# Scale and shift of the last layer norm: from GpSimd on the rows to ScalarE behind the transposes

## The reference

```python
xn = (x - mu) * rsqrt(var + EPS) * gamma + beta      # last norm, over D = 256, 6250 rows
logits = xn @ Wr + br                                # router, 8 experts
w = softmax(top_2(logits))
for e in range(8):                                   # every row only needs its two experts
    h = gelu(xn @ W1[e] + b1[e])                     # 256 -> 512
    y += (h @ W2[e] + b2[e]) * w_full[..., e]        # 512 -> 256
x = x + y
```

## Time and profile before

| what | value |
|---|---|
| time, median of 3 runs | 5023.93 us (5022.15 to 5025.44) |
| the profiled execution, its own time | 5019.38 us |
| its span, first to last instruction | 5017.7 us |
| mean granted TensorE clock | 0.823 |
| busy: PE, DVE, ACT, POOL | 64%, 59%, 39%, 56% of the span |
| heads stage | starts at 4020.1 us |
| experts stage, PE at work | from 4365.0 us |

### The profile page before, as it was taken

One profiled execution on the slowest core, in us unless ns is written; L12 is line 12 of the kernel. 1 busy time (PEld: TensorE's weight loads), 2 busy tenths in 40 slices (PEclk: granted clock), 3 DMA queues, 4 the chain that ended last, 5 costly groups with the idle time before them and its releaser, 6 DMA issues. The chain is left out here.

```text
span 5017.7 us, 69695 instructions
## 1 busy us (share of the span) xinstructions
PE 3229.1 (64%) x14347; PEld 2350.6 (47%) x14348; DVE 2974.7 (59%) x7138; ACT 1979.9 (39%) x4909; POOL 2789.1 (56%) x2929
## 2 busy tenths in 40 slices
PE   4477777777566677777798246666666532199980
PEld 1255555555454555555587134444444431066650
DVE  5677777777667777777547855555555592022223
ACT  0434444443333344444342045555555452133331
POOL 0277777677477677777450067777777645400006
PEclk9978878888778788888899668888888755599995
DMA  2433333333233333333221011111111332511115
GB/s 81 141 113 115 117 110 111 111 110 108 85 108 109 95 108 110 110 110 111 68 68 44 7 25 27 27 27 27 27 27 27 22 145 92 181 56 54 55 57 145
DMA packets 265988, 410.61 MB, mean 82 GB/s; under 512 B 77510, under 2 KB 182883, under 8 KB 265508
## 3 DMA queue, kind: packets, MB, share of 16 engines
q0 software_dynamic: 120320, 275.83, 20.6%
q1 hardware_dynamic: 145444, 132.39, 8.3%
HBM read 324.85 MB, written 83.11 MB: 81 GB/s over the span
## 5 line engine op out<-in xcount | busy, mean ns | idle before, releaser
L1482 PE MATMUL conv_ps<-conv_msg,conv_S 128*128 128x256 f32 x3328 | 1068.7, 468 | 408.5 <-DVE ACC L1492 320.8
L1482 PEld LDWEIGHTS conv_ps<-conv_msg,conv_S 128*128 128x128 f32 x3328 | 727.7, 232 | 658.3 <-DVE ACC L1492 326.7
L1458 POOL DMA_INDIRECT conv_msg<-relu_xn_table,GI x832 | 789.9, 949 | 382.9 <-issue 248.3
L1458 POOL DMA_INDIRECT conv_msg<-conv_table,GI x832 | 796.5, 957 | 326.6 <-issue 249.0
L2399 POOL DMA_INDIRECT gat_msg<-attn_table,GI x832 | 821.7, 988 | 266.2 <-issue 253.4
L1492 DVE TENSOR_TENSOR ACC<-ACC,conv_ps 128x256 f32 x1664 | 701.8, 422 | 411.8 <-issue 247.3
L2452 PE MATMUL gat_ps<-gat_M,gat_S 128*128 128x260 f32 x1664 | 598.9, 509 | 374.6 <-DVE ACC L2506 221.0
L1467 ACT ACTIVATE conv_S<-iota_row,LOC 128x128 f32<-128x128 f32 x1664 | 507.3, 388 | 530.3 <-PE conv_ps L1482 521.0
L2452 PEld LDWEIGHTS gat_ps<-gat_M,gat_S 128*128 128x128 f32 x1664 | 378.9, 246 | 517.6 <-issue 460.4
L3060 POOL DMA_INDIRECT combine_y<-expert_out,combine_at x98 | 94.6, 966 | 578.3 <-ACTq L3048 559.1
L2506 DVE TENSOR_TENSOR ACC<-ACC,gat_ps 128x260 f32 x832 | 349.7, 420 | 56.5 <-PE gat_ps L2452 23.4
(11 more groups left out here) (537 smaller groups left out, 5420.2 us busy)
## 6 DMA issues: line engine op xcount, KB each, us to landing
expert_in<-heads_zrow SPq DMA_DIRECT2D x53, 256.0 KB, 3.1
experts_xe<-expert_in SPq DMA_DIRECT2D x106, 128.0 KB
expert_out<-experts_y SPq DMA_DIRECT2D x106, 128.0 KB
conv_msg<-relu_xn_table,GI POOLq DMA_INDIRECT x832, 2.8
conv_msg<-conv_table,GI POOLq DMA_INDIRECT x832, 2.7
gat_msg<-attn_table,GI POOLq DMA_INDIRECT x832
relu_xn_table<-begin_rx SPq DMA_DIRECT2D x49, 128.0 KB, 1.7
xnT<-begin_xt SPq DMA_DIRECT2D x49, 128.0 KB, 1.8
```

The lines of the kernel that those rows point to most:

```text
L1458: pool.indirect_dma_start(self.msg[:, h * RING + k, :], None, table, bass.IndirectOffsetOnAxis(ap=self.m.GI[:, t:t + 1], axis=0)).then_inc ...
L1482: self.nc.tensor.matmul(self.ps[k % self.NB][:, 0:D], self.S[:, r % 2, k, :], self.msg[:, r % self.DEEP * RING + k, :], start=True, stop=T ...
```

## The change

`gamma` and `beta` are loaded once, as two columns of 128 (`m.gammac`, `m.betac`), in the load stage. In heads, ScalarE writes the normalised rows `xn`, which are transposed and written to DRAM without scale and shift; GpSimd keeps only the fill with zeros. Once transposed, a column of the row is a partition, so `gamma` and `beta` are per-partition operands: ScalarE's one copy of 128x256 from PSUM becomes two activations of 128x128 with scale and bias from `gammac` and `betac`. The same is done in the experts stage, whose input now comes without scale and shift. The wait for the write of a row buffer moves from GpSimd to ScalarE.

```diff
 # stage_load
-            for to, frm in ((m.b11s, m.b11), (m.b21s, m.b21)):
+            for to, frm in ((m.b11s, m.b11), (m.b21s, m.b21), (m.gammac, m.gamma), (m.betac, m.beta)):
                 load(to[:, :], frm.rearrange("(c p) -> p c", p=P), allow_slow_non_contiguous=True)
 # heads, ScalarE
                     if i >= TS:
-                        act.wait_ge(u_made, i - TS + 1)
-                    nc.scalar.activation(t[:, i % TS, :], x_of(i), ACT.Identity, scale=m.rstd[:, i:i + 1],
-                                         bias=shift[:, i:i + 1]).then_inc(t_made, 1)
+                        act.wait_ge(turned, i - TS + 1)
+                        act.wait_ge(out_xn[i % TS], i // TS * 16)
+                    nc.scalar.activation(xn[:, i % TS, :], x_of(i), ACT.Identity, scale=m.rstd[:, i:i + 1],
+                                         bias=shift[:, i:i + 1]).then_inc(xn_made, 1)
...
-                    nc.scalar.copy(xt[:, i % TS, :], pt[i % 2][:, 0:D]).then_inc(xt_made, 1)
+                    for c in range(2):
+                        op = nc.scalar.activation(xt[:, i % TS, c * P:c * P + P], pt[i % 2][:, c * P:c * P + P], ACT.Identity,
+                                                  scale=m.gammac[:, c:c + 1], bias=m.betac[:, c:c + 1])
+                    op.then_inc(xt_made, 1)
 # heads, GpSimd
             nc.gpsimd.memset(zrow[:, :], 0.0).then_inc(zeroed, 1)
-            pool.wait_ge(scales_in, 32)
-            for j in range(TILES + 1):
...
-                    nc.gpsimd.tensor_tensor(u[:, j % TS, :], t[:, j % TS, :], gammar[:, :], ALU.mult).then_inc(u_made, 1)
...
-                        pool.wait_ge(turned, i - TS + 1)
-                        pool.wait_ge(out_xm[i % TS], i // TS * 16)
-                    nc.gpsimd.tensor_tensor(xm[:, i % TS, :], u[:, i % TS, :], betar[:, :], ALU.add).then_inc(xm_made, 1)
 # heads, TensorE: wait xn_made, transpose xn;  SyncE:
-            sp.dma_start(gammar[:, :], row_to_all(m.gamma)).then_inc(scales_in, 16)
-            sp.dma_start(betar[:, :], row_to_all(m.beta)).then_inc(scales_in, 16)
...
-                sp.wait_ge(xm_made, i + 1)
-                sp.dma_start(m.xm[i * P:(i + 1) * P, :], xm[:, i % TS, :]).then_inc(out_xm[i % TS], 16)
+                sp.wait_ge(xn_made, i + 1)
+                sp.dma_start(m.xm[i * P:(i + 1) * P, :], xn[:, i % TS, :]).then_inc(out_xn[i % TS], 16)
 # experts, ScalarE
-                nc.scalar.copy(xt[s][:, :], pt[s][:, 0:D]).then_inc(xt_made, 1)
+                for c in range(2):
+                    op = nc.scalar.activation(xt[s][:, c * P:c * P + P], pt[s][:, c * P:c * P + P], ACT.Identity,
+                                              scale=m.gammac[:, c:c + 1], bias=m.betac[:, c:c + 1])
+                op.then_inc(xt_made, 1)
```

More of the change, by code:

```diff
@@ L2563, in stage_heads_to_router @@
         a, b, q, root, shift = (st.sb(n, [P, TILES]) for n in ("a", "b", "q", "root", "shift"))
-        t, u, xm, xt = (st.sb(n, [P, TS, D]) for n in ("t", "u", "xm", "xt"))
+        xn, xt = (st.sb(n, [P, TS, D]) for n in ("xn", "xt"))
         zrow = st.sb("zrow", [P, 2 * D])
-        gammar, betar = st.sb("gammar", [P, D]), st.sb("betar", [P, D])
-        scales_in = st.sem("scales_in")
         pt = [st.ps(f"pt{k}") for k in range(2)]
         pl = st.ps("pl")
-        o_made, low_made, ex_made, o_read, x_made, var_made, root_made, scaled, t_made, u_made, xm_made = (
-            st.sem(n) for n in ("o_made", "low_made", "ex_made", "o_read", "x_made", "var_made", "root_made", "scaled",
-                                "t_made", "u_made", "xm_made"))
+        o_made, low_made, ex_made, o_read, x_made, var_made, root_made, scaled, xn_made = (
+            st.sem(n) for n in ("o_made", "low_made", "ex_made", "o_read", "x_made", "var_made", "root_made", "scaled", "xn_made"))
         turned, xt_made, l_made, zeroed, zero_out = (st.sem(n) for n in ("turned", "xt_made", "l_made", "zeroed", "zero_out"))
-        out_xm = st.sems("out_xm", TS)
+        out_xn = st.sems("out_xn", TS)
         block = st.block()
@@ L2674, in _ @@
             nc.gpsimd.memset(zrow[:, :], 0.0).then_inc(zeroed, 1)
-            pool.wait_ge(scales_in, 32)
-            for j in range(TILES + 1):
-                if there(j):
-                    pool.wait_ge(t_made, j + 1)
-                    nc.gpsimd.tensor_tensor(u[:, j % TS, :], t[:, j % TS, :], gammar[:, :], ALU.mult).then_inc(u_made, 1)
[L2680 to L2683, removed]
-                        pool.wait_ge(turned, i - TS + 1)
-                        pool.wait_ge(out_xm[i % TS], i // TS * 16)
-                    nc.gpsimd.tensor_tensor(xm[:, i % TS, :], u[:, i % TS, :], betar[:, :], ALU.add).then_inc(xm_made, 1)
         @block.tensor
@@ L2691, in _ @@
                 if there(j):
-                    pe.wait_ge(xm_made, j + 1)
+                    pe.wait_ge(xn_made, j + 1)
                     if j >= 2:
@@ L2695, in _ @@
                     for c in range(2):
-                        tr = nc.tensor.transpose(pt[j % 2][:, c * P:c * P + P], xm[:, j % TS, c * P:c * P + P], m.ident[:, :])
+                        tr = nc.tensor.transpose(pt[j % 2][:, c * P:c * P + P], xn[:, j % TS, c * P:c * P + P], m.ident[:, :])
                     tr.then_inc(turned, 1)
@@ L2714, in _ @@
             for i in range(TILES):
-                sp.wait_ge(xm_made, i + 1)
-                sp.dma_start(m.xm[i * P:(i + 1) * P, :], xm[:, i % TS, :]).then_inc(out_xm[i % TS], 16)
+                sp.wait_ge(xn_made, i + 1)
+                sp.dma_start(m.xm[i * P:(i + 1) * P, :], xn[:, i % TS, :]).then_inc(out_xn[i % TS], 16)
             for k in range(TS):
-                sp.wait_ge(out_xm[k], 16 * ((TILES + TS - 1 - k) // TS))
+                sp.wait_ge(out_xn[k], 16 * ((TILES + TS - 1 - k) // TS))
             sp.wait_ge(zero_out, 16 * (EX_TILES // 2))
@@ L3211, in gps_program @@
         m.zeros_bf = sb("zeros_bf", [P, 512], BF16)
+        m.gammac, m.betac = sb("gammac", [P, 2]), sb("betac", [P, 2])
         m.rbr = sb("rbr", [P, EXPERTS])
```

## The result

| | before | after |
|---|---|---|
| median of five runs of each, run beside each other | 5022.15 us (5021.41 to 5025.44) | 5045.44 us (5044.13 to 5047.68) |
| ratio after/before, 95% interval | | 1.0045 (1.003 to 1.006) |
| profiled execution, its span | 5019.38, 5017.7 | 5045.76, 5043.7 |

The change makes the kernel 23.3 us slower, 0.45%. The forecast was 5049 with a range of 5036 to 5061.

The account below looks back on a forecast made before the run. VectorE was taken to bound heads, TensorE experts. Experts +46.6, heads -22.5 and load +1.0 sum to +25.1 us: 5044.5 for the profiled execution, 5049 for a median of runs, range 5036 to 5061.

Parts of the forecast that it names:

- The price of the pair: ScalarE's two activations in experts: 0.45 us for one, 0.81 for both, ending 0.44 later than the copy.
- Experts: Experts stage: the copy is last before `ph` in every tile, so 106 tiles grow by 0.44, +46.6 us.
- the sign: Whole kernel: slower or faster, forecast slower by 25.1 us; it turns at a pair delay of 0.27.
- Rival A: Experts: copy not last in tiles the waits don't name; experts cost 23.8, net +2.3, 5026 us; chance 0.05.
- Heads: Heads stage: GpSimd's operations go, VectorE's group falls to 14.54 us, ScalarE becomes the bound: -22.5 us.
- the tail: End of heads: TensorE's 1.37 us a tile sets the pace over ScalarE's 1.21 for 14 tiles, 2.2 us.
- The moved wait: Heads: ScalarE idles once, 4.3 us, before `xn` of tile 4 until the write of tile 0 lands.
- Load: Load stage: two more issues on SP, ahead of the loads of `X`, end it 1.0 us later.
- B: Experts and heads: pair as cheap as with a bias column alone, delay 0.26; net -1.4, 5022.5 us; chance 0.05.
- C: Heads: gains its full 30 us even with the dear pair; net +17.6, 5041.5 us; chance 0.07.
- D: Experts: TensorE's clock falls to its lower level for a tenth of the stage, 5100 us; chance 0.03.
- E: Pair dearer still, 1.08 us for both halves; net +66, 5090 us; chance 0.04.

Follow-up runs that it names:

- no_columns: The kernel after, with the experts' pair of activations given neither scale nor bias column: 5006.31 us in one run.
- one_column: The kernel after, with the experts' pair of activations given the `betac` column alone: 5024.79 us in one run.
- eight_row_buffers: The kernel after, with eight buffers for `xn` instead of four, a semaphore for each: 5043.48 us, 1.0038 of the kernel before.
- gpsimd_idle_work: The kernel after, with GpSimd doing two 128x256 operations a tile in heads on a buffer nobody reads: 5070.35 us, 1.0092 of the kernel before.

## Why the prediction was right

**The price of the pair.** Forecast 0.45 for one, 0.36 between the starts, 0.81 for both, 0.44 more delay than the copy; measured 0.451, 0.81 and 0.44. Working from the row of the same shape and source with one column and adding one column from a pair of rows of another shape held: no_columns and one_column gave 0.09 a column directly. The formula quoted from the Trainium skill (ScalarE: Activation LUTs, What ACT_TABLE_LOAD costs) would have given 0.865 for the pair and 49 us for the stage, and measured are 0.81 and 47.0, so here the row was the better source. Its figure of 93 ns for a per-partition operand is close to the 89 to 90 of these runs.

**Experts.** Forecast +46.6, measured +47.0. That the copy is last before `ph` in every tile, though the waits named it in half of them, was the step on which the sign hung. It held: the gap from its end to `ph` is 0.28 to 0.29 us in the tiles that the waits name and in those that they don't, the kernel after names the pair in 105 of 106, and the four prices give four lengths of a tile without a dead zone. Rival A is out.

**Heads.** Forecast -22.5, measured -25.0. The mechanism was right: GpSimd gone, VectorE back to its clean duration, ScalarE the new bound. From the first `xn` to the end of the last pair the sum said 103.8 us (97.2 of work, 4.3, 2.2, 0.1). Measured are 101.5, from 4053.4 to 4154.8. That the sum came so near is in part luck, since its terms err to both sides. The one that was wrong in its mechanism is the tail. Three terms were off most plainly:

- The pair's hold on ScalarE, taken as 0.72, is 0.68 where nothing waits: 49 x 0.04 = 2.0 too much. With it go the step of 1.84 (1.79) and the group of 15.8 (15.51 by the starts of `low`).
- The tail, 14 tiles x 0.16 = 2.2, where TensorE was to set the pace at 1.37. It does not. Its transposes of the last tiles start at 4150.65, 4151.90 and 4153.09, 1.2 us apart, and follow ScalarE. The 1.37 of the earlier trace rows was the distance of two tiles in a kernel where GpSimd held TensorE, which "where nothing holds it" overlooked: in its last tiles the transposes start some 0.05 after the end of GpSimd's add, also where the profile names no wait (below). The last one, whose row was ready, starts at 4172.56, 0.98 after the one before.
- ScalarE's idle time, forecast as 4.3 in one place, is 5.0 in six: 2.72 behind the write, 0.63, 0.63 and 0.20 in the early steps (4.2 up to there, as forecast), 0.45 and 0.38 in front of the last two pairs.

The three make -2.0 - 2.2 + 0.7 = -3.5 of a difference of -2.3. The rest shows when ScalarE's list is split by instruction, each from its start to the next one's start, or to its own end where a wait follows. The 101.5 us are then 24.6 for `xn` (24.0 forecast), 34.2 for the pairs (35.3, and 0.1 for the end of the last), 22.4 for `low` and `ex` (21.7), 14.9 for table loads and roots (16.2), 5.3 idle (4.3) and nothing for the tail (2.2).

The tail in the kernel before, GpSimd's add, which ends at 4168.39, and the transpose behind it, which starts at 4168.44, 1.37 after the one at 4167.07:

```profile
4167.66 0.73 POOL L2686 TENSOR_TENSOR heads_xm<-heads_u,heads_betar 128x256 f32<-128x256 f32 x1
...
4168.44 0.29 PEld L2696 LDWEIGHTS heads_pt<-ident,heads_xm 128*128 128x128 f32 x2
```

**The moved wait.** It was forecast 39.05 us into the stage, where the write of tile 0 lands (4059.2 of the kernel before). It came at 39.2. eight_row_buffers prices it at 2.9.

**Load.** Forecast +1.0, measured +1.35. The two issues take 0.47 and 0.50 on SP, as the earlier trace rows said. The other 0.35 is scatter as far as the runs tell: SP is 0.68 later already at `b21s` (12.63 against 11.95), ahead of both, and in the other kernels with the two loads the stage ends 0.8 to 1.4 later than before, at 47.6 to 48.3 us.

**Rivals B to E.** B asked for a pair of 0.63, and it is 0.81. C asked for the full 30 in heads; the pair at its real price leaves 25. D asked for a fallen clock, and it was 0.99 over the stage and 1.00 in a stretch of it with TensorE at 87% busy. The stretch:

```profile
4400.00:4500.00 100.00, 87.09 (x349) 56.08 (x348) 21.91 (x39) 36.70 (x77) 0.00 (x0) 1.00 0.16 50
```

E asked for 1.08.

**The sum.** +25.1 forecast; +21.5 in the profiles once the untouched stages' scatter is set aside, and +23.3 between medians. The 3.6 us between forecast and profiles are heads (-2.5), load (+0.35), experts (+0.4), and -1.9 in routing, dispatch and combine, which were costed at nothing. The latter is about the scatter of routing and dispatch, 185.6 to 187.9 us over the runs. The forecast of 5049 stood on a median of 5023.93 before; beside the kernel after it was 5022.15, which is the other part of the distance to 5045.44.

## What to carry to other kernels

Work moved off an engine that crowds another can gain in one stage and lose in the next: multiply each by how often it runs on the path, here 25 us once against 0.44 in each of 106 tiles. When a table of waits names an instruction only in part of the cases, look at the distance from its end to what follows. If that is constant, as 0.28 to 0.29 us was here, it is last in all. And a scale and shift per input column ahead of a product with fixed weights belongs in the weights: folding it once under transfers that run anyway beat both ways of applying it to the rows.

## What the runs showed of the hardware beyond that

- An operation on GpSimd slows VectorE's (0.42 to 0.94 us for 128x256, all in SBUF) even when the two share no data and no semaphore, and it is the order of their starts that decides. In heads of gpsimd_idle_work, between 4050 and 4160 us, 68 of VectorE's operations with two inputs start while one of GpSimd's runs, and each ends 0.28 us after GpSimd's does (4099.85 starts inside 4099.61 to 4100.51 and ends at 4100.79). The 19 that start first, with GpSimd's starting inside them, keep their 0.41 to 0.43 us, as the one at 4103.45 does. `bn_stats`, with one input, takes 0.41 to 0.43 in either case. The Trainium skill (SBUF — State Buffer, SBUF: two separate sides) has a rule for it: GpSimd and VectorE share a pair of ports as an exclusive lock, and between a VectorE operation with two inputs in SBUF and a GpSimd operation that reads SBUF, whichever starts first keeps the pair for its whole length and the other waits. The timeline agrees, save that VectorE's operation needs only 0.28 us more once GpSimd's has ended, not its whole 0.42.
- Prices of columns on VectorE: 128x512 in place in SBUF with one column takes 480 ns, and the addition of two 128x512 tensors, one of them in PSUM, 0.69 us; how much of this difference is the column and how much is PSUM no run tells. From PSUM, 128x128 with two columns takes 410 ns, less than ScalarE's 451.

```profile
L2872 DVE TENSOR_SCALAR W1E<-W1E,gammac x16: 477/480/481, 4312.2 to 4325.6; 128x512 f32<-128x512 f32 x16
```

```profile
L3013 DVE TENSOR_SCALAR experts_xt<-experts_ph,gammac,betac x106: 401/410/413, 4342.3 to 4864.5; 128x128 f32<-128x128 f32 x106
```

- `ph` starts 0.28 to 0.29 us after the last of `xt` in every kernel here, in all but a few tiles. In a convolution of the kernel before, the copy to `conv_hs` ends at 2450.80 and the loads that need it start at 2450.84, some 0.05 later. The loads of `ph` take their expert's address from a register and the others don't. That this is the cause was only argued, not tried.
